# The last sums of an attention and mixture-of-experts kernel on one Trainium2 core: batches 14 and 15 summed a step earlier, gathers released by another event

## Chip, cores and metric

One NeuronCore of one Trainium2 chip. The time is that of the device in microseconds (us) for one execution, as the median of several. A second number is the span of one profiled execution: from its first to its last recorded instruction.

## What is computed

Sixteen batches of 128 tokens, 512 wide, go through a gated cross attention and then a gated feed-forward layer with experts. All is float32. Cut to what matters here:

```python
x = x + tanh(g_xattn) * attention(layernorm(x), ctx, pos)        # 32 heads
xf = layernorm(x)                                                # 2048 tokens x 512
shared_out = (silu(xf @ s1_gate.T) * (xf @ s1_up.T)) @ s2.T      # width 704
probs = softmax(xf @ gate_w.T)                                   # 16 experts
w, e = top_k(probs, 6)
moe_out = sum(w[k] * ((silu(xf @ w1g[e[k]].T) * (xf @ w1u[e[k]].T)) @ w2[e[k]].T) for k in range(6))
x = x + tanh(g_ffn) * (moe_out + shared_out)
```

## The kernel before

The program has two phases. Phase A does the attention and the routing of all 16 batches; it writes each token's normalised row to six places of a DRAM array that is sorted by expert, and writes the token's residual to x1_rows and its normalised row to x2_rows. The change does not touch it.

Phase B is a pipeline of steps. BLOCKS = 111 routed blocks of 128 rows (each of one expert) are followed by SHARED * BATCHES = 32 shared ones: each batch is taken twice, once for each half of the shared expert's width. STEPS is 143, and two more steps drain the pipeline, so the steps are 0 to 144. In step i TensorE does, in this order (`one_step` of `tensor`):

- `down` of block i-2: nine matmuls (L1387) from a_hi, a_lo and the second weights into a PSUM bank. For shared blocks the two of a batch add up in one of three banks.
- `transpose_x` of the tile of block i+1 (L1323), in shared steps every second time
- `transpose_act` of block i-1 (L1364)
- `up` of block i: 24 matmuls, three products for each of four chunks and two halves (L1353), which ends with one more on the count h_mm.

ScalarE follows with x_hi (L1284), a_hi of block i-1 (L1289) and silu of block i (L1295, waits for h_mm). VectorE makes x_lo (L1425), a_lo of block i-1 (L1431, which `down` of the next step waits for) and the product act of block i (L1443, which the transposes of the next step wait for). The float32 operands are split in a high and a low part, hence the pairs of names.

In the routed steps the results go to y_rows in DRAM. When all are there, POOL gathers for each batch its six rows a token with six indirect DMAs (L1268, the loop at L1265) into gath[b % 2], and VectorE adds them up beside the shared products:

- `combine_rows(b)` (L1446): one sum of 128x1536 elements, tree = gath[0:3] + gath[3:6] (L1450). It waits for the six gathers. It is the first of three counts on tree_chain for each batch. After it gath[b % 2] is not read any more.
- `combine(b)` (L1452): two sums within tree and with the residual x1_t (L1456, L1457), and comb[b % 2] (L1459), which counts comb_done.
- `finish(b)` (L1461): the shared products' bank plus comb (L1466), into o_t, which SP stores to the output.

When they run is set by the table `finish_at` (L1137): batch b finishes in step min(111 + 2(b+1) + 5 - b//4, 144). For batches 0 to 15 that is 118, 120, 122, 124, 125, 127, 129, 131, 132, 134, 136, 138, 139, 141, 143, 144. In a step VectorE first does `finish`, then x_lo, a_lo and act, then `combine` of the batch that finishes in the next step, then `combine_rows` of the one that finishes two steps on. Three times (batches 3 and 4, 7 and 8, 11 and 12) two batches finish in neighbouring steps. SP loads x1_t (`load_x1`, L1188) in the step of `combine_rows`, when comb of batch b-2 is made, and stores the output in the step of `finish`.

POOL's gathers of batch b wait until `combine(b-2)` is done (L1266), so batches 0 and 1 wait for nothing but y_rows. Before them POOL splits the weights of the two shared halves.

## Time and profile before

| | us |
|---|---|
| runs, median of 3 | 1582.97 |
| runs, lowest and highest | 1580.36, 1595.71 |
| the profiled execution, its own time | 1586.62 |
| its span | 1584.8 |
| TensorE busy | 1484.9 |
| VectorE, POOL, ScalarE busy | 725.8, 687.2, 495.7 |

The first shared upward product starts at 1351.3 us of the span, the fourth at 1372.9. In the profile an engine's row has its start, how long it took, line, operation and operands, and in brackets how long the engine was idle before it and whose event ended that. The profile calls the engines PE (TensorE; PEld is its weight load), DVE (VectorE), ACT (ScalarE), POOL (GpSimd) and SP (SyncE); "issue" is time for which it shows no cause.

### The profile page before, as it was taken

Reading aid. Unit: us, or ns where it says so; the run is one execution under the profiler, and the core shown is the slowest. Engines: PE = TensorE matmul, PEld = TensorE weight load, DVE = VectorE, ACT = ScalarE, POOL = GpSimd, SP = SyncE. Lnnn points to the kernel's source line nnn. Section 1 sums busy time; section 2 is a strip of 40 time slices with the busy share of each in tenths; the row PEclk is TensorE's granted clock in tenths of the full one; section 3 lists DMA queues with packets and bytes.
Section 4 is the critical chain, followed back from the end, with each engine's and each line's share of the span. In section 5 each row is a group of like instructions: output and inputs, shape, how many; then the busy total and the mean of one; then the engine's idle time right before and its main releaser. Section 6 shows DMA issues by size and latency. Waiting matters only on the chain.

```text
span 1584.8 us, 31992 instructions
## 1 busy us (share of the span) xinstructions
PE 1484.9 (94%) x8922; PEld 1259.4 (79%) x8923; DVE 725.8 (46%) x1555; ACT 495.7 (31%) x982; POOL 687.2 (43%) x1135
## 2 busy tenths in 40 slices
PE   4999999999999937999999999999999999899998
PEld 3666666666666527999999999999999999798896
DVE  4578776776767542222222222222222222145555
ACT  3345443444434302222222222222222222111111
POOL 3457644444443340466442444444344400635554
PEclk8799999999999758999999999999999999999999
DMA  4021522123212235333243343334433232336655
GB/s 181 18 85 72 177 92 71 71 90 111 83 71 75 92 132 175 133 135 118 91 135 135 135 135 130 134 131 133 135 135 135 84 126 81 113 120 199 194 161 171
DMA packets 76009, 190.01 MB, mean 120 GB/s; under 512 B 10451, under 2 KB 12500, under 8 KB 73268
## 3 DMA queue, kind: packets, MB, share of 16 engines
q1 hardware_dynamic: 54260, 99.28, 19.0%
q0 software_dynamic: 21696, 90.06, 16.2%
q8 instruction: 28, 0.46, 0.1%
q14 instruction: 25, 0.20, 0.0%
HBM read 116.80 MB, written 72.50 MB: 119 GB/s over the span
## 4 chain that ended last, share of the span: by engine, by line
PE 76%; DVE 10%; issue 5%; another core or an unknown queue 3%; POOL 2%; ACT 2%; DMA 1%; SPq 1%; DVEq 0%; ACTq 0%; POOLq 0%
PE bank L1353 34%; PE bank L1387 18%; PE bank L616 7%; PE bank L641 5%; PE bank L1323 3%; PE bank L1364 3%; DVE smax L888 3%; PE bank L654 2%; PE bank L623 2%; DVE soft L891 1%; PE bank L671 1%; POOL w_lo L209 1%; ACT soft_t L533 1%; DVE x L936 1%
## 5 line engine op out<-in xcount | busy, mean ns | idle before, releaser
L1353 PE MATMUL bank<-w_hi,x_hi 128*128 (+1 forms) x1144 | 290.8, 335 | 1.6 <-POOL w_lo L209 1.6
L1353 PE MATMUL bank<-w_lo,x_hi 128*128 (+1 forms) x1144 | 278.7, 325 | 0.0
L1353 PE MATMUL bank<-w_hi,x_lo 128*128 (+1 forms) x1144 | 278.7, 325 | 0.0
L205 POOL CAST w_hi<-w_raw 128x352 fp32r<-128x352 f32 x144 | 62.1, 479 | 449.7 <-PE bank L1353 449.7
L1295 ACT ACTIVATE silu<-bank 128x352 f32<-128x352 f32 x143 | 66.5, 465 | 464.8 <-PE bank L1353 429.7
L1443 DVE SCALAR_TENSOR_TENSOR act<-silu,row_w,bank 128x352 f32<-128x352 f32 x111 | 64.4, 581 | 320.0 <-ACT silu L1295 306.0
L1353 PEld LDWEIGHTS bank<-w_lo,x_hi 128*128 128x128 f32 x1144 | 201.1, 189 | 0.0
L1353 PEld LDWEIGHTS bank<-w_hi,x_lo 128*128 128x128 f32 x1144 | 201.0, 189 | 0.0
L1353 PEld LDWEIGHTS bank<-w_hi,x_hi 128*128 128x128 f32 x1144 | 194.4, 190 | 1.9 <-POOL w_lo L209 1.8
L1387 PE MATMUL bank<-w_hi,a_hi 128*128 (+3 forms) x429 | 170.4, 397 | 3.6 <-DVE a_lo L1431 3.6
L1387 PE MATMUL bank<-w_hi,a_lo 128*128 (+3 forms) x429 | 170.1, 397 | 0.0
L1387 PE MATMUL bank<-w_lo,a_hi 128*128 (+3 forms) x429 | 169.7, 396 | 0.0
L1425 DVE TENSOR_TENSOR x_lo<-bank,x_hi 128x512 fp32r<-128x512 f32 x127 | 87.7, 691 | 144.4 <-ACT x_hi L1284 143.8
L527 ACT ACTIVATE soft<-soft 128x512 f32<-128x512 f32 x128 | 80.7, 630 | 228.0 <-DVE soft L891 225.2
L641 PE MATMUL bank<-k_t,q_t 32*128 32x256 f32 x512 | 151.9, 417 | 0.0
L1268 POOL DMA_INDIRECT gath<-y_rows,y_slots x96 | 107.8, 1123 | 98.5 <-DVE comb L1459 72.7
L209 POOL TENSOR_TENSOR w_lo<-w_raw,w_hi 128x352 fp32r<-128x352 f32 x144 | 130.5, 938 | 0.0
L1279 ACT ACTIVATE y<-bank 128x512 f32<-128x512 f32 x111 | 66.3, 597 | 185.5 <-PE bank L1387 185.5
L459 POOL DMA_INDIRECT expert_rows<-row,slots x96 | 94.7, 986 | 64.0 <-DVE slots L996 39.7
L641 PEld LDWEIGHTS bank<-k_t,q_t 32*128 32x128 f32 x512 | 88.7, 192 | 36.6 <-issue 25.5
L888 DVE TENSOR_REDUCE smax<-bank 128x4 f32<-128x512 f32 x128 | 87.8, 686 | 31.5 <-PE bank L641 21.9
L654 PE MATMUL bank<-const,soft 128*128 128x128 f32 x512 | 88.5, 299 | 13.7 <-ACT soft L527 8.8
(184 smaller groups left out, 2388.4 us busy)
## 6 DMA issues: line engine op xcount, KB each, us to landing
xr<-expert_rows SPq DMA_DIRECT2D x111, 264.0 KB
y_rows<-y SPq DMA_DIRECT2D x111, 256.0 KB, 2.0
w_raw<-in_w POOLq DMA_DIRECT2D x18, 1408.0 KB, 6.8
w_raw<-in_w POOLq DMA_DIRECT2D x18, 512.0 KB, 8.1
x_sb<-in_x SPq DMA_DIRECT2D x16, 256.0 KB
x_res<-in_x SPq DMA_DIRECT2D x16, 256.0 KB
x_rows<-x SPq DMA_DIRECT2D x16, 256.0 KB
x_rows<-row SPq DMA_DIRECT2D x16, 256.0 KB, 3.4
```

Of the source, the lines that this page charges most:

```text
L209: nc.gpsimd.tensor_tensor(w1_lo[d][half][:, s], w1_raw[:, d, halves[half]], w1_hi[d][half][:, s].bitcast(F32), ALU.subtract).then_inc(w1_m ...
L459: g.indirect_dma_start(rows, bass.IndirectOffsetOnAxis(slots[j][:, k:k + 1], 0), row[j][:], None)\
L527: a.activation(soft[u % 2][:], soft[u % 2][:], ACT.Exp, scale=SCALE).then_inc(exp_done, 1)
L616: last = nc.tensor.matmul(dst, lhs_at(lhs[l], c), rhs_at(rhs[r], c), start=(n == 0), stop=(n == 3 * chunks - 1))
L641: last = nc.tensor.matmul(bank[2 + u % 2][:, c * 2 * P:(c + 1) * 2 * P], q_t[j][r:r + 32, ch, :], k_t[j][r:r + 32, ch].rearrange("p e n -> ...
L654: last = nc.tensor.transpose(bank[4 + v % 2][:, h * P:(h + 1) * P], soft[v % 2][:, h, :], ident)
L888: v.tensor_reduce(smax[u % 2][:], s3, AX.X, ALU.max).then_inc(smax_done, 1)
L1268: nc.gpsimd.indirect_dma_start(gath[b % 2][:, k, :], None, y_rows, bass.IndirectOffsetOnAxis(y_slots[:, b * 8 + k:b * 8 + k + 1], 0))\
L1295: a.activation(silu[j][:], g_bank[:, 0:WIDTH], ACT.Silu).then_inc(silu_done, 1)
L1353: last = nc.tensor.matmul(to[:, 0:WIDTH], xx[jt][:, d, :], w[d][half][:, cols], start=(d == 0 and xx is x_hi and w is w1_hi), stop=(d == D ...
L1387: last = nc.tensor.matmul(to[:], l[j][0:m, c, :], w[c][0:m, cols], start=(first and c == 0 and k == 0), stop=(final and c == 2 and k == 2))
L1425: v.tensor_tensor(x_lo[j][:].rearrange("p c n -> p (c n)"), x_bank[:], x_hi[j][:].rearrange("p c n -> p (c n)").bitcast(F32), ALU.subtract)\
```

## The change

A second table `sum_at` says in which step `combine(b)` runs: one before `finish(b)` as until now, and for the last two batches two before. `combine_rows(b)` and the load of x1_t run one step before `combine(b)`. So `combine` of batches 14 and 15 is in steps 141 and 142 (before: 142 and 143), their `combine_rows` in steps 140 and 141 (before: 141 and 142). In step 143, `finish(14)` stands behind a_lo instead of ahead of it.

POOL's gathers of batch b from 2 on wait for `combine_rows(b-2)` (the first of its three counts on tree_chain), no longer for `combine(b-2)`. The gathers of batch 1 wait until 115 upward products are done: 111 routed ones and four of the shared stage.

```diff
--- before.py
+++ after.py
@@ -1136,6 +1136,7 @@
 
         finish_at = {min(BLOCKS + SHARED * (b + 1) + (5 - b // 4), STEPS + 1): b
                      for b in range(BATCHES)}
+        sum_at = {finish_at_step - 1 - (b >= BATCHES - 2): b for finish_at_step, b in finish_at.items()}
 
         def tile_of(i):
 
@@ -1219,8 +1220,8 @@
                         load(*at(3))
                     elif t + 2 < TILES:
                         load(t + 2, j, n + 1)
-                if i is not None and i + 2 in finish_at:
-                    load_x1(finish_at[i + 2])
+                if i is not None and i + 1 in sum_at:
+                    load_x1(sum_at[i + 1])
                 if i is not None and i in finish_at:
                     b = finish_at[i]
                     sp.wait_ge(y_done, BLOCKS + b + 1)
@@ -1263,7 +1264,10 @@
             for j in range(2):
                 pool.wait_ge(y_out[j], 16 * ((BLOCKS + 1 - j) // 2))
             for b in range(BATCHES):
-                need(pool, comb_done, b - 1)
+                if b == 1:
+                    pool.wait_ge(h_mm, BLOCKS + 4)
+                if b >= 2:
+                    pool.wait_ge(tree_chain, 3 * (b - 2) + 1)
                 for k in range(TOPK):
                     nc.gpsimd.indirect_dma_start(gath[b % 2][:, k, :], None, y_rows,
                                                  bass.IndirectOffsetOnAxis(y_slots[:, b * 8 + k:b * 8 + k + 1], 0))\
@@ -1469,7 +1473,7 @@
             dve.wait_ge(act_zero, 2)
 
             def one_step(i, at):
-                if i is not None and i in finish_at:
+                if i is not None and i in finish_at and i != STEPS:
                     finish(finish_at[i])
                 if i == 0:
                     meta(0, 0, 0)
@@ -1480,12 +1484,14 @@
                     x_low(*tile(i, at, 1))
                 if live(i, -1):
                     a_low(*at(-1))
+                if i == STEPS:
+                    finish(finish_at[i])
                 if live(i, 0):
                     gated(i, at)
-                if i is not None and i + 1 in finish_at:
-                    combine(finish_at[i + 1])
-                if i is not None and i + 2 in finish_at:
-                    combine_rows(finish_at[i + 2])
+                if i is not None and i in sum_at:
+                    combine(sum_at[i])
+                if i is not None and i + 1 in sum_at:
+                    combine_rows(sum_at[i + 1])
 
             steps(dve, one_step)
```

POOL, where the gathers begin; the rows are of before and then of the changed kernel. gath0 and gath1 are the two buffers; x5 stands for five of the same kind.

```order
L220 TENSOR_TENSOR w2_lo_2<-w2_raw,w2_hi_2 96x512
L1268 DMA gath0<-y_rows,y_slots 128x512 [waits y_out1,y_out0,slot_chain]
L1268 DMA gath0<-y_rows,y_slots 128x512 x5
L1268 DMA gath1<-y_rows,y_slots 128x512 x6
L1268 DMA gath0<-y_rows,y_slots 128x512 [waits comb_done]
```

```order
L220 TENSOR_TENSOR w2_lo_2<-w2_raw,w2_hi_2 96x512
L1272 DMA gath0<-y_rows,y_slots 128x512 [waits y_out1,y_out0,slot_chain]
L1272 DMA gath0<-y_rows,y_slots 128x512 x5
L1272 DMA gath1<-y_rows,y_slots 128x512 [waits h_mm]
L1272 DMA gath1<-y_rows,y_slots 128x512 x5
L1272 DMA gath0<-y_rows,y_slots 128x512 [waits tree_chain]
```

The second batch's six have a wait of their own, and the third batch's wait for tree_chain.

VectorE from act of step 140 to act of step 141, before and then changed. comb1 is batch 13's sum, gath0 batch 14's rows, o_t1 batch 13's output.

```order
L1443 SCALAR_TENSOR_TENSOR act0<-silu0,tanh2,bank2 128x352 [waits a_mm,silu_done]
L1456 TENSOR_TENSOR tree<-tree 128x512 [waits tree_chain,x1_in1]
L1457 TENSOR_TENSOR tree<-tree,x1_t1 128x512
L1459 TENSOR_TENSOR comb1<-tree 128x512 [waits tree_chain]
L1466 TENSOR_TENSOR o_t1<-bank6,comb1 128x512 [waits o_out1,comb_done,y_mm]
L1431 TENSOR_TENSOR a_lo0<-bank3,a_hi0 128x384 [waits a_hi_done]
L1443 SCALAR_TENSOR_TENSOR act1<-silu1,tanh2,bank2 128x352 [waits a_mm,silu_done]
```

```order
L1447 SCALAR_TENSOR_TENSOR act0<-silu0,tanh2,bank2 128x352 [waits a_mm,silu_done]
L1460 TENSOR_TENSOR tree<-tree 128x512 [waits tree_chain,x1_in1]
L1461 TENSOR_TENSOR tree<-tree,x1_t1 128x512
L1463 TENSOR_TENSOR comb1<-tree 128x512 [waits tree_chain]
L1454 TENSOR_TENSOR tree<-gath0 128x1536 [waits comb_done,gathered0]
L1470 TENSOR_TENSOR o_t1<-bank6,comb1 128x512 [waits o_out1,comb_done,y_mm]
L1435 TENSOR_TENSOR a_lo0<-bank3,a_hi0 128x384 [waits a_hi_done]
L1447 SCALAR_TENSOR_TENSOR act1<-silu1,tanh2,bank2 128x352 [waits a_mm,silu_done]
```

The sum over the rows of batch 14 (gath0) stood behind act of step 141 and now stands ahead of batch 13's output sum and the a_lo of step 141.

VectorE from act of step 142 to the end, before and then changed. comb0 and o_t0 are batch 14's, gath1, comb1 and o_t1 batch 15's.

```order
L1443 SCALAR_TENSOR_TENSOR act0<-silu0,tanh2,bank2 128x352 [waits a_mm,silu_done]
L1456 TENSOR_TENSOR tree<-tree 128x512 [waits tree_chain,x1_in0]
L1457 TENSOR_TENSOR tree<-tree,x1_t0 128x512
L1459 TENSOR_TENSOR comb0<-tree 128x512 [waits tree_chain]
L1450 TENSOR_TENSOR tree<-gath1 128x1536 [waits comb_done,gathered1]
L1466 TENSOR_TENSOR o_t0<-bank4,comb0 128x512 [waits o_out0,comb_done,y_mm]
L1431 TENSOR_TENSOR a_lo0<-bank3,a_hi0 128x384 [waits a_hi_done]
L1456 TENSOR_TENSOR tree<-tree 128x512 [waits tree_chain,x1_in1]
L1457 TENSOR_TENSOR tree<-tree,x1_t1 128x512
L1459 TENSOR_TENSOR comb1<-tree 128x512 [waits tree_chain]
L1466 TENSOR_TENSOR o_t1<-bank5,comb1 128x512 [waits o_out1,comb_done,y_mm]
```

```order
L1463 TENSOR_TENSOR comb0<-tree 128x512 [waits tree_chain]
L1454 TENSOR_TENSOR tree<-gath1 128x1536 [waits comb_done,gathered1]
L1435 TENSOR_TENSOR a_lo1<-bank3,a_hi1 128x384 [waits a_hi_done]
L1447 SCALAR_TENSOR_TENSOR act0<-silu0,tanh2,bank2 128x352 [waits a_mm,silu_done]
L1460 TENSOR_TENSOR tree<-tree 128x512 [waits tree_chain,x1_in1]
L1461 TENSOR_TENSOR tree<-tree,x1_t1 128x512
L1463 TENSOR_TENSOR comb1<-tree 128x512 [waits tree_chain]
L1435 TENSOR_TENSOR a_lo0<-bank3,a_hi0 128x384 [waits a_hi_done]
L1470 TENSOR_TENSOR o_t0<-bank4,comb0 128x512 [waits o_out0,comb_done,y_mm]
L1470 TENSOR_TENSOR o_t1<-bank5,comb1 128x512 [waits o_out1,comb_done,y_mm]
```

Between the last act and the last a_lo stood three sums, a row sum and an output sum; now there are three sums (batch 15's). The changed piece begins with batch 14's comb0 and batch 15's row sum, which are in step 141 now.

## Rows read from the trace of the kernel before

**Rows 1.** The page's first part: busy us (share of the span) and instructions.
```profile
PE 1484.9 (94%) x8922; PEld 1259.4 (79%) x8923; DVE 725.8 (46%) x1555; ACT 495.7 (31%) x982; POOL 687.2 (43%) x1135
```

**Rows 2.** Waits of TensorE, then of VectorE, 1340 to 1590 us: total, times, longest.
```profile
PE bank L1364 <- DVE act L1443: 6.5, 3, 4.7
PE bank L1387 <- DVE a_lo L1431: 3.6, 1, 3.6
PE bank L1364 <- issue: 2.0, 1, 2.0
PE bank L1353 <- POOL w_lo L209: 1.6, 1, 1.6
...
DVE tree L1450 <- DMA gath<-y_rows,y_slots: 4.0, 2, 2.2
```

**Rows 3.** TensorE in order of time around the fourth shared upward product: start, us.
```profile
1376.78 0.39 PE L1387 MATMUL bank<-w_hi,a_hi 128*128 128x512 f32 x1
...
1383.78 0.86 PE L1364 MATMUL bank<-const,act 128*128 128x128 f32 x3 [4.73 <-DVE act L1443]
...
1389.59 0.39 PE L1387 MATMUL bank<-w_hi,a_hi 128*128 128x512 f32 x1
```

**Rows 4.** Chain that ended last, in order of time: start us, us.
```profile
1384.64 5.12 PE bank L1353 x24
...
1396.42 2.10 PE bank L1387 x9
...
1402.71 2.10 PE bank L1387 x9
...
1506.74 5.41 PE bank L1353 x24
```

**Rows 5.** ScalarE in order of time, same stretch.
```profile
1382.65 0.46 ACT L1295 ACTIVATE silu<-bank 128x352 f32<-128x352 f32 x1 [8.83 <-remote]
```

**Rows 6.** POOL in order of time: issues of gathers, shared stage.
```profile
1373.20 0.95 POOL L1268 DMA_INDIRECT gath<-y_rows,y_slots  x1 [0.30 <-issue]
...
1406.03 0.94 POOL L1268 DMA_INDIRECT gath<-y_rows,y_slots  x1 [25.63 <-DVE comb L1459]
...
1419.18 0.94 POOL L1268 DMA_INDIRECT gath<-y_rows,y_slots  x1 [4.76 <-DVE comb L1459]
...
1445.29 2.41 POOL L1268 DMA_INDIRECT gath<-y_rows,y_slots  x1 [4.75 <-DVE comb L1459]
...
1467.03 0.95 POOL L1268 DMA_INDIRECT gath<-y_rows,y_slots  x1 [3.92 <-DVE comb L1459]
```

**Rows 7.** VectorE in order of time, last steps.
```profile
1560.54 0.58 DVE L1443 SCALAR_TENSOR_TENSOR act<-silu,tanh,bank 128x352 f32<-128x352 f32 x1 [2.87 <-ACT silu L1295]
...
1563.75 0.55 DVE L1431 TENSOR_TENSOR a_lo<-bank,a_hi 128x384 fp32r<-128x384 f32 x1
...
1572.34 0.58 DVE L1443 SCALAR_TENSOR_TENSOR act<-silu,tanh,bank 128x352 f32<-128x352 f32 x1 [3.23 <-ACT silu L1295]
...
1574.16 0.69 DVE L1459 TENSOR_TENSOR comb<-tree 128x512 f32<-128x512 f32 x1
1574.95 1.76 DVE L1450 TENSOR_TENSOR tree<-gath 128x1536 f32<-128x1536 f32 x1
...
1577.23 0.55 DVE L1431 TENSOR_TENSOR a_lo<-bank,a_hi 128x384 fp32r<-128x384 f32 x1
...
1581.59 0.69 DVE L1466 TENSOR_TENSOR o_t<-bank,comb 128x512 f32<-128x512 f32 x1 [1.89 <-PE bank L1387]
```

**Rows 8.** TensorE in order of time, last steps.
```profile
1561.18 0.55 PE L1364 MATMUL bank<-const,act 128*128 128x128 f32 x3 [0.95 <-DVE act L1443]
...
1565.40 0.39 PE L1387 MATMUL bank<-w_hi,a_hi 128*128 128x512 f32 x1
...
1577.83 0.50 PE L1387 MATMUL bank<-w_hi,a_hi 128*128 128x512 f32 x1 [3.60 <-DVE a_lo L1431]
...
1580.93 0.63 PE L1387 MATMUL bank<-w_hi,a_lo 96*128 96x512 f32 x1
```

## The prediction

> **What bounds the kernel now.** I read the page first: TensorE is busy 94% of the span [rows 1], so only two things can move the end: gaps on TensorE, and what stands behind its last product. The change touches the shared stage alone (the last 34 of 145 steps, from about 1350 us on), so I read the table of waits there next. TensorE waits in it for 13.7 us altogether: 6.5 for activations that VectorE made late (three times, the longest 4.7), 3.6 once for an a_lo, 2.0 once for something the profile does not name, and 1.6 for a weight half from POOL [rows 2]. Everything else of the stage is matmuls back to back: from one group of nine down products to the next it is 6.29 us (1396.42 to 1402.71) in a step without the transposes of x [rows 4].
>
> The longest gap comes early in the stage. After the down products that start at 1376.78 the next instruction of TensorE is at 1383.78, and the next down products start at 1389.59 [rows 3]: 12.81 us where 6.29 is regular, so 6.52 us are lost. The idle time is only 4.73 of it: the upward product behind the gap took 5.12 us, while the regular step leaves under 4.2 beside its 2.10 of down products [rows 4]. ScalarE's row tells what was late: the silu of the fourth shared upward product only at 1382.65 [rows 5], though by the matmuls that product ended where the down products start, at 1376.8. Silu waits for the count of finished upward products and for an old act, nothing else. In that time POOL was issuing the twelve gathers of batches 0 and 1 in one row, the second six from 1373.20 until 1380.40, from where POOL is idle for 25.63 us [rows 6]. Where six stand alone, as from 1406.03 to 1414.42, with a pause of 4.76 before the next at 1419.18, no such gap follows. So my reading is: when more than about eight gathers are under way, the end of a product is seen late. Twelve in a row come again where two batches finish in neighbouring steps, as from 1445.29 until 3.92 before 1467.03 [rows 6]. The other two waits of the 6.5 (1.8 us together, one of them the 0.95 at 1561.18 [rows 8]) and the 2.0 lie in or just behind the three stretches of this kind. The 2.0 is also followed by a slow upward product, 5.41 us from 1506.74 [rows 4].
>
> The last gap is the tail. After the last act VectorE adds batch 14 (three sums up to 1574.85), then the rows of batch 15 (1.76 us), then batch 14's output, and only then a_lo at 1577.23 [rows 7]. The last nine down products wait for it until 1577.83, run slower than before (0.63 us for one, where 0.39 is usual), and end at 1581.56, 3.73 us where 2.10 is regular [rows 4, 8]. The output sum starts at 1581.59 [rows 7], and 2.5 us after its end the span is over.
>
> **The change, part by part.** Term A, the wait before batch 1's gathers. Batch 0's six are issued by 1372.9 (0.30 before 1373.20), the fourth product ends at 1376.8, so the wait holds POOL back by some 4 us, and at that moment batch 0's gathers have largely landed. Behind the waiting instruction stand only the other five gathers of that batch and then batch 2's, and these wait for VectorE anyway, until 1406.03 before the change [rows 6] and now, a step (6.3) and term A (6.5) sooner, about 1393. Six gathers take 7.5 us of POOL, so batch 1's are issued by 1384.6; its first reader comes after 1400, so nothing waits for them. What it removes is the lost 6.52 us, if nothing takes their place. Bounds: 0 from one side (the same delay appears under the moved gathers), -6.5 from the other. I take -6.5, because the pattern six, four to five us of pause, six is what stands from 1406 to 1419 and beyond without a gap in TensorE.
>
> Term B, gathers released by the first sum over the rows instead of the finished sum. From batch 2 on each six start about one step (6.3 us) earlier. VectorE's two waits for gathers (4.0 us [rows 2]) then vanish, but TensorE waited behind neither. The twelve in a row stay: where two batches are summed in neighbouring steps, POOL's 7.5 to 8.5 us of issue fill the step as before, only one step sooner. So I count 0. From below, if all later gaps vanished: -1.8 -2.0 of idle time and -1.6 of the slow product, -5.4. From above, if each of the three later bursts were to cost as much as the first: 3 x 6.5 - 5.4 = +14.1. The nearest rows are the same bursts now, so 0 it is.
>
> Term C, the tail. Batch 15's row sum and batch 14's sums move one step forward, and the output sum of batch 14 behind a_lo. After the last act (1572.34, end 1572.92) VectorE now does three sums, which ended at 1574.85 before, and a_lo can follow at 1574.95 instead of 1577.23, since its only other input, a_hi, follows the last transposes by less: -2.28 [rows 7]. TensorE's idle time falls from 3.60 to 1.3 us. After 4.73, 3.60 and 2.0 of idle time the matmuls turned slow, after 0.95 the next down products came at 1565.40, 4.2 us later, as is regular [rows 8]; I expect 1.3 to leave the pace as it is, so nine down products take 2.10 instead of 3.73: -1.6 (bound 0). Output 14 now stands between a_lo and output 15, but ends by 1576.2, before the products do. C = -3.9, between -2.3 and -3.9.
>
> Term D, what is paid for C. In step 140 VectorE gets 1.76 us of row sum between batch 13's sums and a_lo. Before, act began at 1560.54 and a_lo at 1563.75; now a_lo begins at 1565.5 and ends at 1566.05, while TensorE wants it at 1565.40 [rows 7, 8]: +0.6. If the act is not late itself (it was, by one of the small waits) there is a us more of room and the cost is near 0. I take +0.4, between 0 and 0.7. In step 141 VectorE has three sums and a row sum behind act: a_lo ends at 1571.0, its product is due 6.29 behind 1565.40, at 1571.7, so it is hidden with 0.6 us to spare. If batch 15's gathers land late that cover is gone. They start after batch 13's row sum, which stands behind the act a step before the one at 1560.54, so near 1554.5 by the distance of the steps, and their issue takes up to 8.5 us, to 1563; the row sum comes near 1568.7, so there are over 5 us for landing. The early load of x1 for batch 15 passes one output store on SP's queue and is asked for at the same event as before; 0.
>
> Sum: -6.5 + 0 - 3.9 + 0.4 = -10.0 us. The profiled execution took 1586.6 us (span 1584.8), so it would take 1576.6; against the median of the runs, 1582.97, which is 3.6 below it, the forecast is 1573.0. (About 1%, 16 us, is what a measurement of this kernel can tell from no change.)
>
> A rule that speaks against term A. ScalarE's silu came 5.9 us after its product while gathers ran [rows 3, 5]. The Trainium skill, page "SBUF — State Buffer", section "SBUF: two separate sides", says that the engines' ports and the DMA ports of SBUF are disjoint, so that a transfer and an engine's work cannot slow each other. By that rule the gathers would not be the cause, moving them would buy nothing, and the time would be that of the first rival. The rule speaks of ports and not of how the end of a product is told, and the trace does show a gap of TensorE at each of the four rows of twelve gathers and at no row of six.
>
> **The rivals.** R1: the late silu is not the gathers' doing, or it returns under batch 1's moved gathers, which still follow the first six by only 4 us. For it: no engine rows show how a gather could delay ScalarE. Against: the coincidence above. Then A = 0: -3.5, time 1579.5. R2: the bursts, one step earlier, fall where nothing is late, or the later gaps go with VectorE's waits. Then B = -5.4: -15.4, time 1567.6. For it: the waits for gathers go. Against: twelve in a row stay. R3, the slower one: gathers released earlier crowd together. Batch 7's now follow the twelve of 5 and 6 after about 2.5 us instead of 3.9 [rows 6], and likewise 11 after 9 and 10, and 15 after 13 and 14; eighteen gathers in some 28 us. If the delay grows with the queue, each of the three places costs 6.5 where all three cost 5.4 now, +14.1, and with A, C and D the sum is +4.1, time 1587.1. It decides from 3.3 us a place more than now upward, where the 10.0 are spent. Against it: the pause is only a little shorter. That the change doesn't do what it says, POOL's wait being over when it gets there, would need the fourth product before 1372.9; it ends 4 us later, and a shorter pause is in R1.
>
> **How the numbers follow.** Forecast 0.55, R1 0.27, R2 0.10, R3 0.08. The forecast's own range is 1572.5 to 1577 (the bounds of C and D, and A between the idle 4.7 and 6.5). The range to give reaches over R1 and to the edge of R2: 1568 to 1581, which leaves out R3 and the larger half of R2. Faster by over 1% needs less than 1567.1, half of R2: 0.05. Slower by over 1% needs over 1598.8, a worse R3: 0.01. Within 1%: 0.94.
>
> **What would show it right or wrong.** A: no gap on TensorE between the fourth and fifth shared upward products, and silu about 0.3 us after each. C: a_lo some 2.0 us after the last act's end, the last nine down products in 2.1 us, and the row sum of batch 15 ahead of the last act but one's a_lo. D: at most 0.7 us of idle time before the down products of step 142. B: gathers of batches 2 to 15 begin right behind the row sums, and the later gaps of TensorE again add up to 3 to 5 us. If these gaps are over 10 us, R3 holds; if the first gap is still there, R1.

## The result and the profile after

The changed kernel took 1567.26 us (median of 6 runs, 1563.63 to 1568.23), the kernel before, run beside it, 1583.1 us (6 runs, 1579.94 to 1595.71). The ratio is 0.988, with a 95% interval of 0.985 to 0.991: 15.8 us less. The forecast was 1573.0, the range 1568 to 1581, so the time lies just below the range, where the rival R2 stood (1567.6).

The profiled execution of the changed kernel took 1565.7 us, its span is 1563.8 (before: 1586.6 and 1584.8). The page, share of the span and instructions; it answers to [rows 1]:

```profile
PE 1471.7 (94%) x8922; PEld 1250.2 (80%) x8923; DVE 725.1 (46%) x1555; ACT 495.6 (32%) x982; POOL 678.5 (43%) x1135
```

TensorE is busy 13.2 us less for the same instructions. Matmuls that run at a lower granted clock behind a gap count as busy, so a gap costs more than its idle time (e8 below has the clock behind one).

**Where the 21.0 us of span went.** POOL's last casts of upward weights are the first thing that belongs to the shared stage. First the changed kernel, then the kernel before:

```profile
1344.30 2.17 POOL L205 CAST w_hi<-w_raw 128x352 fp32r<-128x352 f32 x5 [82.70 <-PE bank L1357]
```

```profile
1349.22 2.17 POOL L205 CAST w_hi<-w_raw 128x352 fp32r<-128x352 f32 x5 [82.70 <-PE bank L1353]
```

From their start to the start of the last output sum it is 216.35 us now (1344.30 to 1560.65) and was 232.37 (1349.22 to 1581.59 [rows 7]). I call this distance the shared stage. So 16.0 us were gained in the stage that the change touches; 4.9 us arose before it, in code that is the same in both; I take them as chance of the two executions (the six runs of the changed kernel alone spread over 4.6 us). All comparisons of profiles below use the stage.

The waits of TensorE in the stage (engine and line, what it waited for: us in total, times, longest). They answer to [rows 2]:

```profile
PE bank L1357 <- POOL w_lo L209: 1.6, 1, 1.6
PE bank L1391 <- DVE a_lo L1435: 1.2, 1, 1.2
```

Of 13.7 us, 2.8 are left. All waits for act are gone, and so is the one without a name. VectorE's waits for gathers, 4.0 us before [rows 2], are gone too.

**The early gap.** TensorE from the down products behind the fourth shared upward product, against [rows 3], and ScalarE's fourth silu, against [rows 5]:

```profile
1372.05 0.39 PE L1391 MATMUL bank<-w_hi,a_hi 128*128 128x512 f32 x1
...
1378.34 0.39 PE L1391 MATMUL bank<-w_hi,a_hi 128*128 128x512 f32 x1
```

```profile
1372.25 0.47 ACT L1299 ACTIVATE silu<-bank 128x352 f32<-128x352 f32 x1 [3.34 <-PE bank L1357]
```

From down products to down products it is 6.29 us (1372.05 to 1378.34), where it was 12.81. The fourth silu starts 0.20 us behind its product, where it was 5.87.

POOL's gathers, the first of each six, against [rows 6]; the row at 1434.16 is the sixth of batch 5:

```profile
1360.63 1.05 POOL L1272 DMA_INDIRECT gath<-y_rows,y_slots  x1 [0.17 <-issue]
...
1372.48 0.94 POOL L1272 DMA_INDIRECT gath<-y_rows,y_slots  x1 [4.52 <-PE bank L1357]
...
1388.22 0.94 POOL L1272 DMA_INDIRECT gath<-y_rows,y_slots  x1 [8.56 <-DVE tree L1454]
...
1427.48 0.94 POOL L1272 DMA_INDIRECT gath<-y_rows,y_slots  x1 [5.52 <-DVE tree L1454]
...
1434.16 2.28 POOL L1272 DMA_INDIRECT gath<-y_rows,y_slots  x1 [0.30 <-issue]
...
1446.95 0.94 POOL L1272 DMA_INDIRECT gath<-y_rows,y_slots  x1 [2.67 <-DVE tree L1454]
```

The wait of batch 1 ends with the fourth product and costs POOL 4.52 us, as worked out. Batch 2 starts at 1388.22, which with the 4.9 us by which this execution is ahead is the 1393 that I had worked out. But rows of twelve gathers are still there: from 1427.48 until 2.67 before 1446.95, one with a pause of 1.32 us in its middle (batches 9 and 10), and again one without a pause from 1519.04 (batches 13 and 14). By my reading each of these was to hold the end of a product back. The two without a pause did not. In the row with the pause the silu of the 22nd shared product comes 0.96 us after the down products begin, where 0.20 is usual; TensorE does not wait for it:

```profile
1489.67 0.39 PE L1391 MATMUL bank<-w_hi,a_hi 128*128 128x512 f32 x1
```

```profile
1490.63 0.47 ACT L1299 ACTIVATE silu<-bank 128x352 f32<-128x352 f32 x1 [3.91 <-PE bank L1357]
```

**The tail.** VectorE from act of step 140, against [rows 7], and TensorE from the down products of step 142, against [rows 8]:

```profile
1542.64 0.58 DVE L1447 SCALAR_TENSOR_TENSOR act<-silu,tanh,bank 128x352 f32<-128x352 f32 x1 [2.85 <-ACT silu L1299]
...
1545.25 1.76 DVE L1454 TENSOR_TENSOR tree<-gath 128x1536 f32<-128x1536 f32 x1
...
1547.53 0.55 DVE L1435 TENSOR_TENSOR a_lo<-bank,a_hi 128x384 fp32r<-128x384 f32 x1
...
1555.18 0.58 DVE L1447 SCALAR_TENSOR_TENSOR act<-silu,tanh,bank 128x352 f32<-128x352 f32 x1 [1.42 <-ACT silu L1299]
...
1557.63 0.56 DVE L1435 TENSOR_TENSOR a_lo<-bank,a_hi 128x384 fp32r<-128x384 f32 x1
...
1560.65 0.69 DVE L1470 TENSOR_TENSOR o_t<-bank,comb 128x512 f32<-128x512 f32 x1 [1.86 <-PE bank L1391]
```

```profile
1548.23 0.41 PE L1391 MATMUL bank<-w_hi,a_hi 128*128 128x512 f32 x1
...
1558.25 0.50 PE L1391 MATMUL bank<-w_hi,a_hi 128*128 128x512 f32 x1 [1.17 <-DVE a_lo L1435]
...
1560.22 0.40 PE L1391 MATMUL bank<-w_hi,a_lo 96*128 96x512 f32 x1
```

From the last act to the last output sum it is 5.47 us (1555.18 to 1560.65), where it was 9.25: 3.78 less. The nine last down products take 2.37 us (1558.25 to 1560.62), not 3.73, and the idle time ahead of them is 1.17, not 3.60. The row sum of batch 14 (1545.25) now stands ahead of a_lo of that step, which ends at 1548.08; the down products begin at 1548.23 without a wait.

### The profile page after: what moved, and what is told of

It reads as the page before. It is cut to its first block, busy times and chain, and to the rows that moved or that the text cites. A ratio compares the mean times of both kernels' runs of the same rounds, so it can differ in the third digit from the quotient of the medians.

```text
span 1563.8 us, 31992 instructions
## 1 busy us (share of the span) xinstructions
PE 1471.7 (94%) x8922; PEld 1250.2 (80%) x8923; DVE 725.1 (46%) x1555; ACT 495.6 (32%) x982; POOL 678.5 (43%) x1135
## 4 chain that ended last, share of the span: by engine, by line
PE 75%; DVE 12%; issue 5%; POOL 3%; ACT 2%; another core or an unknown queue 1%; DMA 1%; SPq 1%; DVEq 0%; ACTq 0%; POOLq 0%
PE bank L1357 35%; PE bank L1391 19%; PE bank L616 6%; PE bank L641 4%; PE bank L1327 4%; DVE smax L888 3%; PE bank L1368 3%; PE bank L654 2%; PE bank L623 2%; DVE soft L891 1%; PE bank L671 1%; POOL w_lo L209 1%; ACT soft_t L533 1%; DVE x L936 1%
## 5 line engine op out<-in xcount | busy, mean ns | idle before, releaser
L1272 POOL DMA_INDIRECT gath<-y_rows,y_slots x96 | 99.2, 1034 | 86.3 <-DVE tree L1454 56.6
```

Source lines behind the costliest of these rows:

```text
L1272: nc.gpsimd.indirect_dma_start(gath[b % 2][:, k, :], None, y_rows, bass.IndirectOffsetOnAxis(y_slots[:, b * 8 + k:b * 8 + k + 1], 0))\
```

## The experiments

Call the parts A (batch 1's gathers wait for the fourth product), B (gathers wait for the row sum) and C (the tail). Theory P: these parts make and unmake TensorE's gaps. Rival H: the later gaps follow from the first one. Rival M: the gaps belong to the chip or the execution, not to the code.

**Which chips.** The kernel before was run beside every group of experiments. On three chips it takes 1554.4 to 1555.4 us, on two others 1581.0 and 1596.5; the first pair (1583.1) is like these two. I call them quick and slow chips. The same program differs by up to 42 us between them. The changed kernel's shared stage is the same on both kinds (216.5 us in e6 and e9, 216.35 in the first pair), so what a slow chip loses in the stage are the gaps that the change removes; the rest of its time is lost ahead of the stage.

The size of a difference in the stage rests on one profile of each kernel. Three profiles of e1's kernel on quick chips (e1, e16, e18) gave 221.6, 220.0 and 220.0 us, so less than 1.6 us between two stages says little by itself.

### Parts alone, on a quick chip (before: 1555.3 us)

e1 is part A alone, e2 part B alone, e3 part C alone, e4 A and C. Against the changed kernel, the first two removed lines below take A out, the third with the first added line takes B out, and the rest takes C out.

```diff
-                if b == 1:
-                    pool.wait_ge(h_mm, BLOCKS + 4)
...
-                    pool.wait_ge(tree_chain, 3 * (b - 2) + 1)
+                    pool.wait_ge(comb_done, b - 1)
...
-        sum_at = {finish_at_step - 1 - (b >= BATCHES - 2): b for finish_at_step, b in finish_at.items()}
+        sum_at = {finish_at_step - 1: b for finish_at_step, b in finish_at.items()}
...
-                if i is not None and i in finish_at and i != STEPS:
+                if i is not None and i in finish_at:
...
-                if i == STEPS:
-                    finish(finish_at[i])
```

> Only the wait of batch 1's six gathers for the fourth shared upward product; everything else as in the kernel before. Theory P (what counts is where a row of gathers lies against the step's products): the first gap goes, -6.5 us, and the later gaps of TensorE behind batches 5 and 6, 9 and 10, 13 and 14 stay (3.8 us idle and one slow product), so about 0.996 of before. Theory H (the later gaps follow from the first, through a backlog or a shifted step): all gaps but the tail's go, about -12 us, 0.9925.

> Only the release of the gathers of batches 2 to 15 by the first sum over the rows; batch 1's follow batch 0's without a wait, the sums as before. Theory P: the first gap of 6.5 us stays, the three later ones go, -5.4 us, 0.9966, with no wait of VectorE for gathers. Theory H: nothing goes but what follows the first gap stays too, within 1 us of before.

> Only the earlier sums of batches 14 and 15 and the output sum of 14 behind a_lo; the gathers are released by the finished sum as before. Batch 15's gathers then start a step before their row sum wants them. Theory 1 (the gathers are late then): VectorE waits 5 to 6 us for them in step 141 ahead of a_lo, TensorE idles 4 to 5 us before the down products of step 143, and with the tail's -3.8 the sum is 0 to +1 us. Theory 2 (they land in time): -3.8 us, 0.9976.

> The change without its release of gathers by the row sum. If terms add up: e1 plus e3, so -6.5 plus 0 to +1 under P (0.996 to 0.9965) and -12 under H. Against the whole change (-15.8) the difference is what the release is worth: 9 to 10 us under P with theory 1, 5.4 under P with theory 2.

Measured: ratios to before of 1.000 (0.997 to 1.003), 0.999 (0.995 to 1.002), 1.002 (0.999 to 1.006) and 1.000 (0.997 to 1.003). The stage: 221.6, 220.6, 223.0 and 220.6 us. No silu is late in any of them, although e2 and e3 start with twelve gathers in a row. This could mean that each part is worthless, or that this chip does not show what the first one did; hence the next group.

C alone is no gain, because the row sums move forward and the gathers don't. VectorE's waits for gathers in e3:

```profile
DVE tree L1452 <- DMA gath<-y_rows,y_slots: 13.7, 5, 5.1
```

The kernel before waits 7.8 us in three waits on a quick chip (e5). TensorE then waits 5.7 us for a_lo, which stands behind the late sums, where it waits 3.8 in e5.

### Before, after, and B with C on another quick chip (before: 1554.4 us)

e5 is the kernel before, e6 the changed one, e7 the changed one without A.

> The kernel before, unchanged, profiled again and timed against itself: the ratio is 1 within 0.003. Theory M (the gaps of TensorE behind late products belong to the chip or the execution, not to the order of the gathers): on a chip where e1 to e4 showed none, this kernel shows none either, and VectorE waits 10 to 15 us in all for gathers without costing TensorE anything; the only waits left are 3.6 for the last a_lo and 1.6 for a weight half. Theory P (the order makes them): the four gaps of 8.5 us idle in all are there again.

> The changed kernel, unchanged. Theory M: only the tail's term is worth anything here, -3.8 us, 0.9976 of before, and from the first cast of the last weights to the last output sum it takes some 217 us where e2 takes 220.6. Theory P: -15.8 us, 0.990, as on the first chip.

> The whole change without batch 1's wait for the fourth upward product. Theory M: the same as e6 within 1 us, since e2 had twelve gathers in a row at the start and no gap behind them. Theory P: the first gap of 6.5 us is back.

Measured: 1.000 (0.996 to 1.003), 0.997 (0.995 to 1.000), 0.997 (0.993 to 1.000); stages of 221.2, 216.5 and 216.3 us. TensorE's waits in e5, the kernel before:

```profile
PE bank L1387 <- DVE a_lo L1431: 3.8, 2, 3.6
```

The 3.6 is the tail. Beside it there are only 0.2 us for another a_lo and the 1.6 for a weight half; all other gaps of the first profile are missing from the very same code. VectorE waits 7.8 us for gathers here, more than the 4.0 of the first profile, and nothing is late. Its fourth product and the silu behind it:

```profile
1352.46 0.39 PE L1387 MATMUL bank<-w_hi,a_hi 128*128 128x512 f32 x1
```

```profile
1352.66 0.47 ACT L1295 ACTIVATE silu<-bank 128x352 f32<-128x352 f32 x1 [3.15 <-PE bank L1353]
```

0.20 us, where the first profile had 5.87. So on quick chips M holds: the whole change is worth 4.6 us of the stage (221.2 to 216.5), most of it in the tail, and for it C needs B: e4, which lacks only B, has 220.6. In the times this is 0.997, with an interval that ends at 1.000.

### Before, after, B with C, and B alone on a slow chip (before: 1596.5 us)

> The kernel before, once more, in case this call falls on another chip. Theory P (the order of the gathers against the steps makes TensorE's gaps of the first pair of profiles): the late fourth upward product and the three later gaps are there again, shared stage near 232 us. Theory M (they belong to the chip or the execution): as on the chips of the two calls before, no silu over 1 us late and a shared stage near 221 us; if this chip is a slow one (before near 1580 us), gaps are there in all kernels that keep before's order.

> The changed kernel on the same chip. Theory M on a quick chip: shared stage 216.5 us, ratio near 0.997. On a slow chip (before near 1580 us) both theories expect what the first pair showed: ratio near 0.988 and a shared stage near 216.4 against 232. If the ratio there stays near 0.997, the 11 us of gaps in the first profile were that execution's alone.

> The changed kernel without the second batch's wait, so that the first twelve gathers stand in a row as before. Quick chip: as the changed kernel within 1 us, as it was in e7. Slow chip: if the twelve in a row make the fourth product late (my term A), one gap of 6.5 us between the fourth and the fifth upward product and 6.5 us more than the changed kernel; if the wait is worth nothing there too, the same time.

> Only the release of the gathers by the row sum. Quick chip: within 1 us of before in the shared stage, as in e2 (220.6 us). Slow chip: if the release by the row sum is what took the three later gaps away, shared stage near 226 (first gap kept, 6.5) or less; if not, near 232 as before.

Measured, as ratio and stage: e8 (before) 0.999 (0.996 to 1.002), 237.0 us; e9 (after, four runs only) 0.986 (0.980 to 0.993), 216.6; e10 (B and C) 0.994 (0.990 to 0.998), 223.0; e11 (B) 0.997 (0.994 to 1.001), 226.7. TensorE's waits, of e8, then e11, then e10 (each also has the 1.6 for a weight half):

```profile
PE bank L1387 <- DVE a_lo L1431: 6.4, 2, 3.6
PE bank L1364 <- DVE act L1443: 5.4, 2, 4.8
PE bank L1364 <- issue: 2.8, 1, 2.8
```

```profile
PE bank L1366 <- DVE act L1445: 4.8, 1, 4.8
PE bank L1389 <- DVE a_lo L1433: 3.6, 1, 3.6
```

```profile
PE bank L1366 <- DVE act L1445: 4.7, 1, 4.7
PE bank L1389 <- DVE a_lo L1433: 1.2, 1, 1.2
```

Step by step: B takes 10.3 us (237.0 to 226.7) and with them the wait without a name, the 2.8 of the a_lo waits that is not the tail, and a small one for act. C takes 3.7 (the 3.6 for a_lo becomes 1.2, and the pace behind it). A, added last, takes 6.4 (the 4.7 for act, and the pace). In e9 what is left is exactly what stands above for the changed kernel.

So P holds on slow chips: 20.5 us here, 16.0 in the first pair. A and C agree in size with the first pair (6.5 and 3.8); B does not. Its 10.3 is less sure than the rest. The profiled execution of e8 was the slowest of its eleven runs (1608.9 us, median 1595.0), and the ratios of the run times put some 4.5 us on B, 5.8 on C and 11.7 on A, each with an interval several us wide.

H is not needed, as in e11 the first gap is there and the later ones are not. It is not ruled out: with B in it, e11 may break the link from the first gap to the later ones, and A alone was never run on a slow chip (e1, e16 and e18 all fell on quick ones).

How one late count costs 6.4 us is seen in e8. (The trace has the event of the count itself 0.02 us ahead of the silu, so it is the count that is late and not the silu's other wait, for an old act.) The down products behind the fourth upward product begin on time; the silu that waits for its count comes 5.9 us later, and TensorE runs dry. TensorE, ScalarE, and POOL's last gather of the row:

```profile
1394.62 0.39 PE L1387 MATMUL bank<-w_hi,a_hi 128*128 128x512 f32 x1
...
1401.64 0.69 PE L1364 MATMUL bank<-const,act 128*128 128x128 f32 x2 [4.75 <-DVE act L1443]
```

```profile
1387.96 0.47 ACT L1295 ACTIVATE silu<-bank 128x352 f32<-128x352 f32 x1 [3.37 <-issue]
...
1400.51 0.46 ACT L1295 ACTIVATE silu<-bank 128x352 f32<-128x352 f32 x1 [7.41 <-remote]
```

```profile
1397.13 0.95 POOL L1268 DMA_INDIRECT gath<-y_rows,y_slots  x1 [0.30 <-issue]
```

The windows (us, busy time of PE, PEld, DVE, ACT and POOL, then the granted clock, the DMA share and GB/s) show the clock after the gap:

```profile
1396.00:1400.00 4.00, 0.89 (x4) 0.38 (x2) 0.00 (x0) 0.00 (x0) 1.78 (x2) 1.00 0.73 209
1400.00:1404.00 4.00, 2.36 (x9) 2.36 (x10) 1.14 (x2) 0.96 (x2) 0.00 (x0) 0.71 0.02 8
```

The mean granted clock falls to 0.71 in the window behind the gap, so some matmuls ran at the lower level of 1.2 GHz: 4.75 us idle, and about 1.7 more at that pace (6.4 between e10 and e9). The later gaps have a late silu ahead of them too, as the one in the row of batches 9 and 10, with its silu and the first and last issue of the row:

```profile
1528.61 0.90 PE L1364 MATMUL bank<-const,act 128*128 128x128 f32 x3 [2.84 <-issue]
```

```profile
1527.48 0.46 ACT L1295 ACTIVATE silu<-bank 128x352 f32<-128x352 f32 x1 [6.94 <-remote]
```

```profile
1514.00 2.42 POOL L1268 DMA_INDIRECT gath<-y_rows,y_slots  x1 [5.32 <-DVE comb L1459]
...
1529.26 1.79 POOL L1268 DMA_INDIRECT gath<-y_rows,y_slots  x1 [0.30 <-issue]
```

This silu comes while the row is still being issued, 3.6 us before the last issue ends, and so does that of the same row in the first profile (1505.06, with the last issue until 1509.94). The silu of the first row comes 2.43 us after its last issue (1398.08).

### How many gathers in a row, and where (a third slow chip, before: 1581.0 us)

Each is the changed kernel with another wait in the first two batches: e12 lets eight go before the wait, e13 ten, and in e14 all twelve wait for the fourth product.

For e13 (e12 has 2 for 4):

```diff
-                if b == 1:
-                    pool.wait_ge(h_mm, BLOCKS + 4)
...
                 for k in range(TOPK):
+                    if b == 1 and k == 4:
+                        pool.wait_ge(h_mm, BLOCKS + 4)
```

For e14:

```diff
-                if b == 1:
+                if b == 0:
                     pool.wait_ge(h_mm, BLOCKS + 4)
```

> The changed kernel, but two of the second batch's six gathers go at once, so eight stand in a row before the wait for the fourth shared upward product. If that product's count is late when more than about eight are under way (my reading of the first profile), it is in time or late by less than 2 us here, and the shared stage stays near 216.5 us. If the number under way decides nothing and only the last gather of the whole row must follow the product, the same; if already two more are enough, the count is late and the silu behind the fourth product starts when the eight have landed, some 12 to 13 us after the first gather. On a quick chip (before near 1555 us) nothing is late whatever the number.

> The same with ten in a row. Theory 'held until the row has landed': a fourth silu late by about 3 to 4 us on a slow chip, when the ten have landed, 14.5 to 15 us after the first gather (with twelve it came 17.3 us after the first in all four profiles that show it), and a TensorE gap of 2 to 3 us. Theory 'only a row of twelve': nothing late. Quick chip: nothing late.

> The changed kernel, but both first batches' gathers wait for the fourth product, so twelve stand in a row two steps later than before. Theory 'number under way': on a slow chip the fifth or sixth upward product's silu is late by up to 6 us and comes 17.3 us after the first gather. Theory 'place': the row of twelve is harmless there as the later ones were in the changed kernel, and nothing is late. Quick chip: nothing late.

Measured: 0.992 (0.988 to 0.996), 0.992 (0.988 to 0.995), 0.997 (0.995 to 0.999); stages of 216.2, 218.4 and 221.9 us. (The stage of the changed kernel is 216.3 to 216.6.) For e12, the down products behind the fourth product and the silu:

```profile
1378.98 0.39 PE L1391 MATMUL bank<-w_hi,a_hi 128*128 128x512 f32 x1
```

```profile
1379.24 0.47 ACT L1299 ACTIVATE silu<-bank 128x352 f32<-128x352 f32 x1 [2.52 <-PE bank L1357]
```

For e13, the first and the tenth gather, the product's end (the down products behind it) and the silu:

```profile
1374.52 1.05 POOL L1272 DMA_INDIRECT gath<-y_rows,y_slots  x1 [0.17 <-issue]
...
1385.91 0.95 POOL L1272 DMA_INDIRECT gath<-y_rows,y_slots  x1 [0.30 <-issue]
```

```profile
1385.93 0.39 PE L1391 MATMUL bank<-w_hi,a_hi 128*128 128x512 f32 x1
```

```profile
1388.82 0.46 ACT L1299 ACTIVATE silu<-bank 128x352 f32<-128x352 f32 x1 [5.30 <-remote]
```

For e14, the first and the twelfth gather, and again product and silu:

```profile
1381.36 1.05 POOL L1272 DMA_INDIRECT gath<-y_rows,y_slots  x1 [12.43 <-PE bank L1357]
...
1395.28 0.95 POOL L1272 DMA_INDIRECT gath<-y_rows,y_slots  x1 [0.30 <-issue]
```

```profile
1393.26 0.39 PE L1391 MATMUL bank<-w_hi,a_hi 128*128 128x512 f32 x1
```

```profile
1398.45 0.46 ACT L1299 ACTIVATE silu<-bank 128x352 f32<-128x352 f32 x1 [5.97 <-remote]
```

| | gathers in the row | silu behind its product | last issue's end to silu | stage |
|---|---|---|---|---|
| e12 | 8 | 0.26 | 1.63, held by the product itself | 216.2 |
| e13 | 10 | 2.89 | 1.96 | 218.4 |
| e14 | 12, two steps later | 5.19 | 2.22 | 221.9 |
| e8 | 12 | 5.89 | 2.43 | 237.0, later gaps too |

With ten and with twelve the silu comes 2.0 to 2.4 us after the last issue of the row ended, wherever the row stands. From the first gather it is 14.3 us in e13 (expected 14.5 to 15) and 17.1 in e14 (expected 17.3). By then the row has all but landed. The DMA engines move data until e8's silu and none in the 2.5 us behind it (last columns: share and GB/s). In e14 it is 213 GB/s before 1398.5 and 0 after, in e13 195 before 1389.25 and 0 after.

```profile
1398.00:1400.50 2.50, 0.00 (x0) 0.00 (x0) 0.00 (x0) 0.00 (x0) 0.08 (x1) 1.00 0.64 188
1400.50:1403.00 2.50, 1.36 (x6) 1.36 (x7) 0.58 (x1) 0.88 (x2) 0.00 (x0) 0.73 0.00 0
```

So "place" falls for the row of the first two batches. That the gathers hold the count there is shown, by one profile each: two or four of them more in the row move the silu. For this row it holds that the count of a product that ends late in it is held until the row has been issued and has all but landed. It is no rule for every row: in the kernel before, the count in the row of batches 9 and 10 comes while the row still runs. With eight, all were issued when the product ended, so a threshold of eight is not shown. Nor is it every product in a row: in e8 the third silu (1387.96) is on time, 4.8 us after the first gather (1383.21).

### The later rows broken up (quick chips both times)

e15 and e17 are e1's kernel with the ninth gather of two later rows of twelve waiting for a product; e16 and e18 are e1's kernel.

```diff
                 for k in range(TOPK):
+                    if b in (6, 10) and k == 2:
+                        pool.wait_ge(h_mm, BLOCKS + (16 if b == 6 else 23))
```

> Before plus the second batch's wait, and in two of the three later rows of twelve (batches 5 and 6, 9 and 10; not 13 and 14) the ninth gather waits for the next but one upward product, so that eight stand in a row, then four; the release by the finished sum stays as before. Slow chip, theory 'a row of over eight without a pause holds the counts back': nothing late in the two broken rows, the late silu and the gap in the third row stay, shared stage 4 to 7 us under that of e16. Theory 'the release by the row sum itself is what matters' (VectorE's order, not the pauses it gives): the silus of the two broken rows are as late as in e16, and the stage the same or longer. Quick chip: the same as e16 within 1 us.

> Before plus the second batch's wait alone. Slow chip: no gap behind the fourth product; late silus of 2 to 4 us in each of the three later rows of twelve, shared stage 6.4 us under that of the kernel before, near 226 (first chip) to 230 us (chip of e8). Quick chip: 221.6 us as in e1.

> As e15, which fell on a quick chip. Slow chip, theory 'pauses in the row': nothing late in the two broken rows, a late silu and a gap in the row of batches 13 and 14, shared stage 4 to 7 us under that of e18. Theory 'order on VectorE': silus as late as in e18 in all three rows. Quick chip: nothing late, the same stage as e18 within 1 us, and the question stays open.

> Base of e17. Slow chip: no late fourth product, late silus of 2 to 4 us in each of the three later rows of twelve, shared stage 226 to 230 us. Quick chip: near 221 us.

Measured: e15 0.999 (0.995 to 1.003) and 221.5 us of stage, e16 0.998 (0.995 to 1.002) and 220.0; e17 1.000 (0.996 to 1.004) and 221.4, e18 0.999 (0.995 to 1.003) and 220.0. Nothing is late in any, as on every quick chip. The stage with the break is 1.4 to 1.5 us longer than without it, where at most 1 was expected; since e1's kernel itself gave 221.6 once, a cost of the break is not shown. On the question these runs tell nothing, and it stays open.

## Why the prediction was wrong, point by point

**Term B, 0: this is the step that failed.** It said "The twelve in a row stay", and "So I count 0". They do stay, but the gaps go. B is worth 10.3 us by the profiles of e8 and e11, on a slow chip (some 4.5 by their run times). In the first pair it is what A and C leave of the 16.0: -6.5 for the early gap (12.81 became 6.29) and -3.78 for the tail, so -5.7 for B; I had given -5.4 as its lower bound and the value of R2. For the first pair the bound was worked out rightly from the waits and the slow product, and the value taken between the bounds was wrong. In e8 the later gaps are larger and the bound does not hold. I took it from the rows of twelve alone, which are the same in number, and not from what else changes in them: VectorE no longer waits for gathers in the stage, each row starts a step earlier, and in the changed kernel slow issues stand in the middle of a row (2.28 us for the sixth of batch 5) or a pause does. The rows of before have slow issues as well (2.41 us for the first of batch 5 [rows 6], 2.27 for the fourth of batch 6), at other places. Which of these keeps the counts in time was not shown, so the cause of B's gain stays open. Nor is B worth nothing on quick chips: with A and C it is 4.1 us of the stage (e4 against e6), because the tail needs its gathers a step sooner.

**Term A, -6.5: right in size where it acts.** 6.4 us between e10 and e9, and 6.5 in the first pair. The wait of POOL was 4.52 us, and nothing waited for the moved gathers. The reading behind it, "when more than about eight gathers are under way, the end of a product is seen late", is right in sign and wrong as a rule: ten and twelve in an unbroken row do it at the start of the stage (e13, e14), two later unbroken rows of twelve in the changed kernel do not, and on quick chips none does.

**Term C, -3.9: right.** -3.78 in the first pair, -3.7 between e11 and e10. That the products keep their pace after a short wait was right as well: 2.37 us for the nine after 1.17 of idle time, near the 2.10 and far from 3.73. That C needs B I had only as a remark on late gathers; e3 shows it, 1.9 us longer in the stage than the kernel before in e5, as much as TensorE waits longer for a_lo (5.7 against 3.8).

**Term D, +0.4: 0.** The act of step 140 was not late this time (the small wait for it is gone), which I had named as the case with near 0.

**R1** (A = 0) is what the quick chips show, and there the rule on ports that I had taken from the Trainium skill (page "SBUF — State Buffer", section "SBUF: two separate sides") goes with the right outcome. On slow chips the conclusion I drew from it fails: the number of gathers in the first row sets how late the silu is (0.26, 2.89, 5.19 us behind its product), so the gathers are the cause. The rule itself is not touched: what is late is a count, not an operand. **R2** is what happened in the first pair: 1567.6 said, 1567.26 measured. It had 0.10, which was too little. That it agrees to 0.4 us is in part luck: its B of -5.4 came close here, and on the chip of e8 B was 10.3. Its argument (VectorE's waits go) is not shown to be the reason: in e5 VectorE waits 7.8 us for gathers and no count is late. **R3** did not happen: batch 7's gathers follow the twelve after 2.67 us and nothing is late behind them.

**The range.** It left R2's larger half out on purpose. The unknown that I did not see is larger than all terms together: on another chip the same change gives 0.997 instead of 0.988, because the gaps that it removes are not there.

## What to carry to other kernels

A long gap behind an instruction that had long been issued may be a count that is told late, and here, on slow chips, a row of ten or twelve indirect gathers did that. Such a row can be broken up at the end of a product: at the start of the stage that was worth 6.4 us on a slow chip and cost nothing clear of the scatter on a quick one (216.5 with it, 216.3 without). Price a gap with what follows it, not by its idle time (4.75 us idle were 6.4 us lost). Before a gap in one profile is taken as the kernel's property, look whether another execution on another chip has it, and compare profiles by the stage that the change touches, since 4.9 of the 21.0 us of span lay outside it.

## What the runs showed of the hardware that was not expected

- The same program takes 1554 to 1555 us on three chips, and 1581 to 1597 on two others and in the first pair. Late counts of over 2 us are only on the second kind, in six of nine profiles (not in the changed kernel's two and e12), and in none of eleven on the first. Those three have the 22nd silu 0.8 to 0.9 us late; on quick chips none is late at all.
- The two kinds differ in what is recorded as well. In all eleven profiles of quick chips the trace has when the gathers landed (median 3.8 to 4.3 us from the issue), in none of the nine of slow chips does it, because about half of their landing events are missing. All times here are of recorded executions. So it is not known whether counts are late on a slow chip also when nothing is recorded, and this rival was not tested.
- On slow chips the end of a product reaches ScalarE up to 5.9 us late while TensorE's own next instructions run on. In the row of the first two batches it comes 2.0 to 2.4 us after the last gather was issued; in the later row of batches 9 and 10 it comes while gathers are still being issued.
- The chance between executions of one kernel is wide (the kernel before beside e8: 1588 to 1616 us in 25 runs; beside e5, on a quick chip: 1549 to 1565 in 29); what of it lies ahead of the shared stage, as the 4.9 us of the first pair do, was not studied.
